# Transposes of 28 layer norm tiles: from TensorE to transposing transfers in SyncE's queue

## The chip, the cores and the metric

The kernel runs on the 8 cores of one Trainium2 chip. Each core computes one of the 8 batch items by itself; the cores exchange nothing. The metric is the device time of the slowest core in microseconds (us). The engines of a core are TensorE (PE; its weight loads are listed as PEld), VectorE (DVE), ScalarE (ACT), GpSimd (POOL) and SyncE (SP), which here only issues transfers (DMA).

## What is computed

For each batch item x of 2048 rows and 1024 columns: a gated feed-forward with half weight, an attention block with random features and its own MLP, and the same feed-forward again, each with a layer norm ahead of it.

```python
def _layernorm(x, axis=-1, eps=1e-5):
    m = jnp.mean(x, axis=axis, keepdims=True)
    v = jnp.var(x, axis=axis, keepdims=True)
    return (x - m) / jnp.sqrt(v + eps)
...
        gate = jnp.einsum('bsd,hd->bsh', x, wg)
        up = jnp.einsum('bsd,hd->bsh', x, wu)
        h = jax.nn.silu(gate) * up
        return jnp.einsum('bsh,dh->bsd', h, wd)

    x = x + 0.5 * _L0_ffn_ref(_layernorm(x, axis=-1), L0_ffn_w_gate, ...)
    x = x + _L0_attn_ref(_layernorm(x, axis=-1), ...)
    x = x + 0.5 * _L0_ffn_ref(_layernorm(x, axis=-1), L0_ffn_w_gate, ...)
    return x
```

Inside the attention block: q, k, v are x times Wq, Wk, Wv; q and k become exponential features of width 128 per head; a running state over the sequence gives the attention; then Wo, a residual, a second (inner) norm with gamma and beta, and relu(h W1 + b1) W2 + b2.

## The kernel before

**Tiling.** x stays in SBUF for the whole run as 16 tiles of 128 rows (x_tm). The 16 tiles are four blocks of 4 tiles (512 rows). Every matmul has a 512-wide right side, either 512 rows of activations with the features on the partitions (column groups: gate, up, q, k, w1) or 512 columns of weights (row groups: down, v, wo, w2).

**Norms.** Each block has three norms ahead of its three parts: LN1, LN2, LN3; besides, the inner norm of the attention block (called I). A tile of LN1, LN2 or LN3 passes through four steps. DVE takes statistics (L266 to L269, about 1.5 us) and POOL turns the variance into rstd. DVE writes the normalised tile in bf16 into one of the two halves of lntm (L297). PE transposes it in eight 128 x 128 pieces into one PSUM bank (L305). ACT copies the bank into its place in fmX, fmY or fmZ (L314), which is the activation operand of the next part. The tiles are numbered m = 0 to 47 in the order ln_order; a tile's half of lntm is m % 2, so normalisation m waits until tile m - 2 has been transposed (s_ltr). A part waits for the copies of its four tiles (s_lev).

**Weights.** All weights stream through a ring of 8 slots of 512 KB. SyncE issues the load of slot n when PE is done with slot n - 8 (sp_program, L699), one queue, in order. PE uses a slot for 16 matmuls, about 3.5 us, so a load is issued some 27 us ahead of its use. After three of the down parts SyncE also stores the four output tiles of a block.

**Order of the work.** Each engine has one hand-written program. A part of one block is the main stream on PE (gu, down, w1, w2, q, wo, k and v); side() is called after each group of matmuls and gives one tick to a side job: the attention steps of another block, norm tiles, or the inner norm. The same tick numbers are used on PE, DVE and ACT, with offsets, so that the engines meet. LN2 of blocks 1 to 3 is a side job inside the attention ticks (LN_STEP, one tile each at steps 29, 37, 45 and 53), where its transposes borrow the bank of the scores. LN3 of blocks 0 and 1 runs beside wo(1) and wo(2); LN3 of block 2 beside w1(3), of block 3 beside gu of block 2. After wo(b) comes kv_part(b + 1), beside which the inner norm I of block b is taken: dve_i_tick (statistics, then L355), pe_i_tick (transposes, L366, from the tick 5 of kv_part), act_i_tick (L375).

The evictions of wo(b) are on DVE (L1172, 8 per part, each 0.7 us); PE cannot start bank t of the next part before eviction t of the second half.

Of the kernel before, what the change touches and what calls it, by code (L numbers as in the profile page):

```python
# [40 lines left out]
def build():  # L41
# [29 lines left out]
    with es:  # L71
# [3 lines left out]
        def sem(name):  # L75
            return es.enter_context(nc.semaphore(name))
# [56 lines left out]
        s_lxf, s_ltr, s_lev = sem("s_lxf"), sem("s_ltr"), sem("s_lev")  # L133
        s_ixf, s_itr, s_iev = sem("s_ixf"), sem("s_itr"), sem("s_iev")
# [17 lines left out]
        def slot(n):  # L152
# [10 lines left out]
                    "I3", "32", "33"]  # L163

# [126 lines left out]
        def dve_ln_xform(e, which, b, j):  # L291
            n = st_no(which, b) + j
            m = ln_no(which, b) + j
            e.wait_ge(s_rstd, n + 1)
            if m >= 2:
                e.wait_ge(s_ltr, m - 1)
            e.tensor_scalar(lntm[:, (m % 2) * 1024:(m % 2 + 1) * 1024], xt(b * 4 + j),  # L297
                            mv[:, 2 * n:2 * n + 1], rstd[:, n:n + 1],
                            ALU.subtract, ALU.mult).then_inc(s_lxf, 1)

# [275 lines left out]
        def pe_attn(e, b, s):  # L576
            i, t0 = s // 2, 32 * b
            if s % 2 == 0:
                if i < 32:
                    pe_proj(e, t0 + i)  # L580
                if 0 <= i - 3 < 32:

                    if s - 1 in LN_STEP and b < 3:
                        e.wait_ge(s_lev, ln_no(LN2, b + 1) + LN_STEP.index(s - 1) + 1)
                    pe_scores(e, t0 + i - 3)
            else:
                if i >= 8 and i % 4 == 0:
# [12 lines left out]
                if s in LN_STEP and b < 3:  # L600
                    e.wait_ge(s_am, t0 + min(i - 2, 32))
                    pe_ln_transpose(e, LN2, b + 1, LN_STEP.index(s), 2)

        def act_attn(e, b, s):
            i, t0 = s // 2, 32 * b
            if s % 2:
                if i < 32:
                    act_exp(e, t0 + i)
            else:
                if 0 <= i - 2 < 32:  # L610
                    act_fme(e, t0 + i - 2)
                if i >= 9 and (i - 1) % 4 == 0:
                    act_oev(e, 8 * b + (i - 1) // 4 - 2)
                if s - 1 in LN_STEP and b < 3:
                    if s - 1 == LN_STEP[0]:
                        e.wait_ge(*((s_v, 16), (s_v, 32), (s_up, 120))[b])
                    act_ln_evict(e, LN2, b + 1, LN_STEP.index(s - 1), 2)
# [32 lines left out]
        def sp_program(e):  # L650
# [25 lines left out]
            store_at[first + 36 + 32 + 16 + 36 + 16 + 4 + 16 + 32 + 36 + 12] = 2  # L676
            for n in range(SL_GU2, len(slots)):
# [21 lines left out]
                e.dma_start(slot(n), src).then_inc(s_ld[n % RING], 16)  # L699
                if n in store_at:  # L700
# [86 lines left out]
        def pe_program(e):  # L787
# [73 lines left out]
            def gu(which, b, xT, side):  # L861
                e.wait_ge(s_lev, ln_no(which, b) + 4)
                for i in range(N_GU):
                    pair(next_slot(), xT, side)
# [4 lines left out]
            def q_part(b, xT, side):  # L869
                e.wait_ge(s_lev, ln_no(LN2, b) + 4)  # L870
# [82 lines left out]
            wo(1, Ticks(lambda k: pe_ln_tick(e, LN3, 0, k, 0, 1)))  # L953
# [9 lines left out]
            wo(2, Ticks(lambda k: pe_ln_tick(e, LN3, 1, k, 0, 1)))  # L963
# [17 lines left out]
        def act_program(e):  # L981
# [87 lines left out]

            def third(b, k):  # L1070
                if k == 0:
                    e.wait_ge(s_w1, 32 * (b + 1))
                act_ln_tick(e, LN3, b, k, 0, 1)
            idle(8, Ticks(lambda k: third(0, k)))
# [11 lines left out]
            idle(8, Ticks(lambda k: third(1, k)))  # L1086
# [11 lines left out]
            e.wait_ge(s_up, 144)  # L1098
            w1(3, Ticks(lambda k: act_ln_tick(e, LN3, 2, k, 0, 2)))
            e.wait_ge(s_w1, 96)  # L1100
            side = Ticks(lambda k: act_ln_tick(e, LN3, 3, k, 0, 4))
            gu(side)
            idle(24, side)
            gu(quiet)

        def dve_program(e):
# [123 lines left out]
            wo(1, Ticks(lambda k: dve_ln_tick(e, LN3, 0, k, 0, 1)))  # L1230
            side = Ticks(lambda k: dve_i_tick(e, 1, k))
# [10 lines left out]
            wo(2, Ticks(lambda k: dve_ln_tick(e, LN3, 1, k, 0, 1)))  # L1242
            side = Ticks(lambda k: dve_i_tick(e, 2, k))
# [122 lines left out]
```

## Time and profile before

| | us |
|---|---|
| median of 3 runs | 1841.48 |
| the runs | 1839.5, 1841.48, 1939.56 |
| the profiled execution, its own time | 1839.98 |
| its span on the slowest core (core 3) | 1838.3 |
| spans of the 8 cores | 1833.1 to 1838.3 |
| PE busy | 1798.1 (98%) |
| DVE busy | 777.5 (42%) |
| ACT busy | 533.1 (29%) |
| POOL busy | 186.3 (10%) |

How to read it: the span goes from the first to the last instruction of a core; the time around it (1.7 us here) belongs to the run and not to any instruction. PE's busy time is the union of its matmuls; their recorded durations overlap, so the cost of a few instructions is read from when the next one starts. A row of a timeline gives start, duration, engine, line, operation, tiles, form and count, and in brackets the idle time of the engine before it with what ended it. Times of a timeline count from the start of the span.

### The profile page before, as it was taken

How to read it: one execution, taken by the hardware profiler on the slowest of the kernel's cores; microseconds unless marked ns; L12 is line 12 of the kernel's file. 1: busy time of each engine (PE TensorE's matmuls, PEld its weight loads, DVE VectorE, ACT ScalarE, POOL GpSimd, SP SyncE). 2: the span in 40 equal slices, each digit the busy share in tenths (PEclk: the TensorE clock that was granted, in tenths of full speed). 3: DMA queues.
4: the chain of work that ended last, by engine and by line, in shares of the span. 5: the costliest groups of instructions: out<-in, count | busy, mean ns of one | idle time of the engine just before them, and what ended most of it. 6: DMA issues, size and time to landing. Idle time of an engine off the chain costs nothing.

```text
span 1838.3 us, 31579 instructions; the slowest of 8 cores (1833.1 to 1838.3 us)
## 1 busy us (share of the span) xinstructions
PE 1798.1 (98%) x10096; PEld 879.3 (48%) x10096; DVE 777.5 (42%) x1697; ACT 533.1 (29%) x1138; POOL 186.3 (10%) x354
## 2 busy tenths in 40 slices
PE   4999999999999999999999999999999999999999
PEld 2444444444445445554454454455554444444444
DVE  4443116511676345655554333566443120442331
ACT  2221002202454246543332541334352141120110
POOL 3111101100011131113000000300000200000000
PEclk9999999999999999999999999999999999999999
DMA  9999986999876843334444544443354444444643
GB/s 202 234 201 191 195 195 157 194 192 191 209 177 172 189 150 127 116 127 138 144 135 136 173 138 139 141 141 131 129 182 147 145 145 156 151 151 151 195 156 107
DMA packets 82235, 296.32 MB, mean 161 GB/s; under 512 B 9632, under 2 KB 9760, under 8 KB 82080
## 3 DMA queue, kind: packets, MB, share of 16 engines
q1 hardware_dynamic: 69552, 249.16, 41.3%
q0 software_dynamic: 12240, 44.11, 17.4%
q8 instruction: 90, 1.47, 0.3%
q10 hardware_dynamic: 288, 1.05, 0.2%
q14 instruction: 65, 0.53, 0.1%
HBM read 311.12 MB, written 52.43 MB: 198 GB/s over the span
## 4 chain that ended last, share of the span: by engine, by line
PE 94%; DMA 2%; DVE 1%; issue 1%; ACT 1%; POOL 0%; DVEq 0%; ACTq 0%; POOLq 0%; SPq 0%
PE d_ps L811 35%; PE d_ps L851 31%; PE d_ps L828 18%; PE a_ps L923 2%; PE d_ps L923 2%; DMA ring<-gu_b 2%; PE a_ps L451 1%; PE a_ps L305 1%; PE a_ps L498 1%; PE a_ps L412 1%; DMA x_tm<-xin 1%; PE a_ps L413 1%; PE a_ps L463 0%; PE a_ps L524 0%; ACT ftm L430 0%
## 5 line engine op out<-in xcount | busy, mean ns | idle before, releaser
L851 PE MATMUL d_ps<-ring,big 128*128 128x512 bf16 x2176 | 487.4, 379 | 0.8 <-DVE th_t L1116 0.7
L851 PEld LDWEIGHTS d_ps<-ring,big 128*128 128x128 bf16 x2176 | 207.1, 98 | 233.5 <-issue 2.3
L991 ACT ACTIVATE th_t<-d_ps 128x512 f32<-128x512 f32 x192 | 115.4, 601 | 590.6 <-PE d_ps L811 590.6
L811 PE MATMUL d_ps<-fmX,ring 128*128 128x512 bf16 x1152 | 266.4, 382 | 4.2 <-DMA ring<-gu_b 2.8
L811 PE MATMUL d_ps<-fmZ,ring 128*128 128x512 bf16 x1152 | 256.3, 379 | 0.0
L1116 DVE SCALAR_TENSOR_TENSOR th_t<-th_t,d_ps 128x512 f32<-128x512 f32 x192 | 131.8, 686 | 232.1 <-ACT th_t L991 232.0
L430 ACT ACTIVATE ftm<-a_ps,nmax 128x128 bf16<-128x128 f32 x512 | 146.9, 371 | 231.7 <-DVE nmax L420 231.7
L811 PEld LDWEIGHTS d_ps<-fmZ,ring 128*128 128x128 bf16 x1152 | 110.6, 98 | 125.6
L811 PE MATMUL d_ps<-fmY,ring 128*128 128x512 bf16 x768 | 169.2, 379 | 1.4 <-ACT fmY L314 1.4
L811 PEld LDWEIGHTS d_ps<-fmX,ring 128*128 128x128 bf16 x1152 | 109.6, 98 | 126.5 <-issue 8.6
L828 PE MATMUL d_ps<-fmX,ring 128*128 128x512 bf16 x640 | 144.9, 379 | 0.0
L828 PE MATMUL d_ps<-fmY,ring 128*128 128x512 bf16 x640 | 144.1, 379 | 0.0
L1121 DVE SCALAR_TENSOR_TENSOR big<-d_ps,th_t 128x512 bf16<-128x512 f32 x168 | 116.2, 692 | 49.4 <-PE d_ps L811 43.1
L1023 ACT ACTIVATE big<-d_ps,b1c_s 128x512 bf16<-128x512 f32 x128 | 88.8, 694 | 134.1 <-PE d_ps L828 133.7
L420 DVE TENSOR_REDUCE nmax<-a_ps 128x4 f32<-128x512 f32 x128 | 88.0, 687 | 87.6 <-PE a_ps L413 87.3
L811 PEld LDWEIGHTS d_ps<-fmY,ring 128*128 128x128 bf16 x768 | 75.0, 98 | 91.4 <-issue 1.5
L490 POOL CAST sb<-Sf 128x130 bf16<-128x130 f32 x120 | 38.9, 324 | 704.7 <-PE a_ps L529 635.0
L828 PEld LDWEIGHTS d_ps<-fmX,ring 128*128 128x128 bf16 x640 | 60.7, 98 | 67.0
L828 PEld LDWEIGHTS d_ps<-fmY,ring 128*128 128x128 bf16 x640 | 60.6, 98 | 66.8
L473 ACT COPY ffm<-a_ps 128x512 bf16<-128x512 bf16 x128 | 76.3, 596 | 38.5 <-PE a_ps L529 36.8
L1148 DVE SCALAR_TENSOR_TENSOR x_tm<-d_ps,x_tm 128x512 f32<-128x512 f32 x48 | 32.6, 689 | 118.7 <-PE d_ps L851 118.4
L1014 ACT ACTIVATE qkv<-d_ps 128x512 bf16<-128x512 f32 x64 | 38.3, 598 | 150.8 <-PE d_ps L828 150.8
(89 smaller groups left out, 1561.0 us busy)
## 6 DMA issues: line engine op xcount, KB each, us to landing
ring<-gu_b SPq DMA_DIRECT2D x144, 512.0 KB, 3.3
ring<-w_b SPq DMA_DIRECT2D x128, 512.0 KB, 3.2
ring<-d_b SPq DMA_DIRECT2D x72, 512.0 KB, 3.2
w_b<-w_f POOLq DMA_DIRECT2D x32, 512.0 KB, 9.3
ring<-gu_i POOLq DMA_DIRECT2D x24, 512.0 KB, 16.8
gu_b<-ring SPq DMA_DIRECT2D x24, 512.0 KB, 16.4
ring<-q_b SPq DMA_DIRECT2D x16, 512.0 KB, 4.1
ring<-k_b SPq DMA_DIRECT2D x16, 512.0 KB, 6.0
```

Source lines behind the costliest of these rows:

```text
L420: e.tensor_reduce(nmax[:, (t % 2) * 4:(t % 2) * 4 + 4], P_PS[:, :].rearrange("p (a b) -> p a b", a=4), axis=AX.X, op=ALU.max, negate=True) ...
L430: r = e.activation(ftm[:, o + j * 128:o + (j + 1) * 128], P_PS[:, j * 128:(j + 1) * 128], AF.Exp, bias=nmax[:, (t % 2) * 4 + j:(t % 2) * 4 ...
L473: e.copy(ffm[:, o:o + 512], T_BF[:, 0:512]).then_inc(s_fme, 1)
L490: e.tensor_copy(state_of(sb, t), state_of(Sf, t)).then_inc(s_sb, 1)
L811: r = e.matmul(d_ps[bank][:, :], ring[:, so + g * 1024 + k * 128:so + g * 1024 + (k + 1) * 128], xT[:, k * 512:(k + 1) * 512], start=(k == ...
L828: r = e.matmul(d_ps[bank][:, :], ring[:, so + j * 1024 + k * 128: so + j * 1024 + (k + 1) * 128], xT[:, k * 512:(k + 1) * 512], start=(k = ...
L851: r = e.matmul(d_ps[t][:, :], lhs[:, o:o + 128], ring[:, so + i * 512:so + (i + 1) * 512], start=(s == 0 and i == 0), stop=(s == n_slots - ...
L923: r = e.matmul(acc[:, :], (big, qkv)[t // 4][:, o:o + 128], ring[:, so + i * 512:so + (i + 1) * 512], start=(s == 0 and i == 0), stop=(s = ...
L991: e.activation(th_t[:, (n % 2) * 512:(n % 2 + 1) * 512], d_ps[2 * (n % 2)][:, :], AF.Tanh, scale=TANH_SC).then_inc(s_tanh, 1)
L1023: e.activation(big[:, f * 512:(f + 1) * 512], d_ps[f % 4][:, :], AF.Relu, bias=b1c[:, f:f + 1]).then_inc(s_relu, 1)
L1116: e.scalar_tensor_tensor(th_t[:, o:o + 512], th_t[:, o:o + 512], 1.0, d_ps[2 * (n % 2)][:, :], ALU.add, ALU.mult).then_inc(s_gm, 1)
L1121: e.scalar_tensor_tensor(dst, d_ps[2 * (n % 2) + 1][:, :], H_SC, th_t[:, o:o + 512], ALU.mult, ALU.mult).then_inc(s_h, 1)
```

## The change

From tile m = 20 on (XBAR0), that is for LN2 of blocks 1, 2 and 3 and for LN3 of all blocks, 28 tiles, the normalised tile is no longer transposed by PE and copied by ACT. SyncE issues one transfer from the half of lntm into the tile's place in fmX, fmY or fmZ, with transpose=True. These transfers stand in SyncE's queue of weight loads, each behind a load with a fixed number (turn_at). Ahead of each, SyncE waits until the tile is normalised (s_lxf), and for the first of a block also until the destination is free. Two new semaphores, one for each half of lntm (s_xb), count their landing; normalisation m waits on them instead of s_ltr, and the part that reads the tiles waits for both instead of s_lev. Tiles 0 to 19 stay as they were. In wo(1) and wo(2) DVE's ticks of the norm have stride 2 instead of 1, and reach into kv_part, where the ticks of the inner norm start in the same call.

```diff
+        XBAR0 = 20
...
             e.wait_ge(s_rstd, n + 1)
-            if m >= 2:
+            if m >= XBAR0 + 2:
+                e.wait_ge(s_xb[m % 2], 16 * ((m - XBAR0) // 2))
+            elif m >= 2:
                 e.wait_ge(s_ltr, m - 1)
...
+        def sp_ln_transpose(e, which, b, j):
+            m = ln_no(which, b) + j
+            dst = ln_order[m // 4][2]
+            e.wait_ge(s_lxf, m + 1)
+            if j == 0:
+
+                e.wait_ge(*((s_v, 16), (s_v, 32), (s_w1, 32), (s_up, 120), (s_w1, 64),
+                            (s_up, 144), (s_w1, 96))[m // 4 - XBAR0 // 4])
+            e.dma_start(dst[:, :].rearrange("p (k t) -> p k t", k=8)[:, :, j * 128:(j + 1) * 128],
+                        lntm[:, (m % 2) * 1024:(m % 2 + 1) * 1024],
+                        transpose=True).then_inc(s_xb[m % 2], 16)
+
+        def pe_ln_wait(e, which, b):
+            m = ln_no(which, b)
+            if m < XBAR0:
+                e.wait_ge(s_lev, m + 4)
+            else:
+                for j in range(2):
+                    e.wait_ge(s_xb[j], 32 * ((m - XBAR0) // 4 + 1))
...
-                    if s - 1 in LN_STEP and b < 3:
-                        e.wait_ge(s_lev, ln_no(LN2, b + 1) + LN_STEP.index(s - 1) + 1)
                     pe_scores(e, t0 + i - 3)
...
-                if s in LN_STEP and b < 3:
-                    e.wait_ge(s_am, t0 + min(i - 2, 32))
-                    pe_ln_transpose(e, LN2, b + 1, LN_STEP.index(s), 2)
...
-                if s - 1 in LN_STEP and b < 3:
-                    if s - 1 == LN_STEP[0]:
-                        e.wait_ge(*((s_v, 16), (s_v, 32), (s_up, 120))[b])
-                    act_ln_evict(e, LN2, b + 1, LN_STEP.index(s - 1), 2)
...
+            turn_at = {}
+            for which, b, at in ((LN2, 1, (105, 110, 114, 118)), (LN2, 2, (156, 160, 164, 168)),
+                                 (LN3, 0, (180, 181, 182, 183)), (LN2, 3, (217, 225, 232, 240)),
+                                 (LN3, 1, (264, 265, 266, 267)), (LN3, 2, (348, 349, 350, 351)),
+                                 (LN3, 3, (380, 382, 384, 386))):
+                for j in range(4):
+                    turn_at[at[j]] = (which, b, j)
...
                 e.dma_start(slot(n), src).then_inc(s_ld[n % RING], 16)
+                if n in turn_at:
+                    sp_ln_transpose(e, *turn_at[n])
...
             def gu(which, b, xT, side):
-                e.wait_ge(s_lev, ln_no(which, b) + 4)
+                pe_ln_wait(e, which, b)
...
-            wo(1, Ticks(lambda k: pe_ln_tick(e, LN3, 0, k, 0, 1)))
+            wo(1, quiet)
...
-            w1(3, Ticks(lambda k: pe_ln_tick(e, LN3, 2, k, 0, 2)))
+            w1(3, quiet)
...
-            wo(1, Ticks(lambda k: dve_ln_tick(e, LN3, 0, k, 0, 1)))
-            side = Ticks(lambda k: dve_i_tick(e, 1, k))
+            side = Ticks(lambda k: (dve_ln_tick(e, LN3, 0, k, 0, 2),
+                                    dve_i_tick(e, 1, k - 8)))
+            wo(1, side)
             idle(8, side)
             v_part(2, side)
```

ACT's ticks for these tiles (act_ln_tick, act_ln_evict) go in the same way, and wo(2) changes like wo(1).

PE's order in the second half of wo(1), first before and then with the change (the tile names are those of the code; L851 and L878 are the same matmul of row_groups):

```order
L851 MATMUL d_ps<-ring,fmZ 128x512 x15
L305 MATMUL a_ps<-ident,lntm 128x128 [waits s_lev,s_lxf]
L305 MATMUL a_ps<-ident,lntm 128x128 x7
L851 MATMUL d_ps<-ring,fmZ 128x512 [waits s_ld6,s_y]
L851 MATMUL d_ps<-ring,fmZ 128x512 x3
L851 MATMUL d_ps<-ring,fmZ 128x512 [waits s_y]
L851 MATMUL d_ps<-ring,fmZ 128x512 x3
L305 MATMUL a_ps<-ident,lntm 128x128 [waits s_lev,s_lxf]
```

```order
L878 MATMUL d_ps<-ring,fmZ 128x512 x15
L878 MATMUL d_ps<-ring,fmZ 128x512 [waits s_ld6,s_y]
L878 MATMUL d_ps<-ring,fmZ 128x512 x3
L878 MATMUL d_ps<-ring,fmZ 128x512 [waits s_y]
L878 MATMUL d_ps<-ring,fmZ 128x512 x3
```

The groups of eight transposes that stood between the matmuls are gone, with their waits for s_lxf and s_lev.

DVE's order in wo(1), from the first normalisation (L297, L303 after) of LN3 of block 0 to the first statistics of the inner norm; L1172 and L1187 are the evictions of wo. Before:

```order
L297 TENSOR_SCALAR lntm<-x_tm,mv,rstd 128x1024 [waits s_rstd,s_ltr]
L1172 SCALAR_TENSOR_TENSOR big<-x_tm,rstd,d_ps 128x512 [waits s_w2,s_rstd,s_wo]
L1172 SCALAR_TENSOR_TENSOR big<-x_tm,rstd,d_ps 128x512 [waits s_rstd,s_wo]
L266 BN_STATS bst<-x_tm 128x6 [waits s_w2x]
L267 BN_STATS bst<-x_tm 128x6
L269 BN_AGGR mv<-bst 128x2 [waits s_bst]
L297 TENSOR_SCALAR lntm<-x_tm,mv,rstd 128x1024 [waits s_rstd,s_ltr]
L1172 SCALAR_TENSOR_TENSOR big<-x_tm,rstd,d_ps 128x512 [waits s_rstd,s_wo] x2
L297 TENSOR_SCALAR lntm<-x_tm,mv,rstd 128x1024 [waits s_rstd,s_ltr] x2
L1172 SCALAR_TENSOR_TENSOR big<-x_tm,rstd,d_ps 128x512 [waits s_rstd,s_wo] x4
L266 BN_STATS bst<-big 128x6 [waits s_y]
```

And with the change, from the first evictions on:

```order
L1187 SCALAR_TENSOR_TENSOR big<-x_tm,rstd,d_ps 128x512 [waits s_rstd,s_wo] x3
L270 BN_STATS bst<-x_tm 128x6 [waits s_w2x]
L271 BN_STATS bst<-x_tm 128x6
L273 BN_AGGR mv<-bst 128x2 [waits s_bst]
L303 TENSOR_SCALAR lntm<-x_tm,mv,rstd 128x1024 [waits s_rstd,s_xb1]
L270 BN_STATS bst<-x_tm 128x6 [waits s_w2x]
L271 BN_STATS bst<-x_tm 128x6
L273 BN_AGGR mv<-bst 128x2 [waits s_bst]
L303 TENSOR_SCALAR lntm<-x_tm,mv,rstd 128x1024 [waits s_rstd,s_xb0]
L1187 SCALAR_TENSOR_TENSOR big<-x_tm,rstd,d_ps 128x512 [waits s_rstd,s_wo] x4
L303 TENSOR_SCALAR lntm<-x_tm,mv,rstd 128x1024 [waits s_rstd,s_xb1]
L270 BN_STATS bst<-big 128x6 [waits s_y]
```

Normalisations 1 and 2 move behind all four evictions of the first half, with a tile's statistics ahead of each, and normalisation 3 moves behind the last eviction, directly ahead of the inner norm's statistics.

SyncE's order with the change around LN3 of block 0 (L724 is the weight load that was L699; before, nothing stood between the loads):

```order
L724 DMA ring<-v_b 128x2048 [waits s_wo]
L316 DMA_TRANSPOSE fmX<-lntm 128x8x128 [waits s_lxf,s_w1]
L724 DMA ring<-v_b 128x2048 [waits s_wo]
L316 DMA_TRANSPOSE fmX<-lntm 128x8x128 [waits s_lxf]
L724 DMA ring<-v_b 128x2048 [waits s_wo]
L316 DMA_TRANSPOSE fmX<-lntm 128x8x128 [waits s_lxf]
L724 DMA ring<-v_b 128x2048 [waits s_wo]
L316 DMA_TRANSPOSE fmX<-lntm 128x8x128 [waits s_lxf]
L724 DMA ring<-gu_b 128x2048 [waits s_qk] x4
```

Each transposing transfer stands behind one v_b load and ahead of the next load, which goes out only after the transfer's own waits.

## Rows read from the trace of the kernel before

**Rows 1.** The page's first part: span, and busy time by engine.

```profile
span 1838.3 us, 31579 instructions; the slowest of 8 cores (1833.1 to 1838.3 us)
PE 1798.1 (98%) x10096; PEld 879.3 (48%) x10096; DVE 777.5 (42%) x1697; ACT 533.1 (29%) x1138; POOL 186.3 (10%) x354
```

**Rows 2.** Waits: engine, line, waited for: us in total, times, longest; last, a line's group.

```profile
PE a_ps L305 <- DVE lntm L297: 24.3, 4, 21.0
PE d_ps L811 <- DMA ring<-gu_b: 2.8, 2, 2.4
...
L498 PE MATMUL a_ps<-ffm 128*128 128x128 bf16 x256 | 35.1, 219 | 2.2 <-ACT fmX L314 1.2 <-ACT fmY L314 1.0
```

**Rows 3.** Busy time by engine, PE's clock, DMA share and GB/s, 515 to 1620 us.

```profile
515.00:1620.00 1105.00, 1097.75 (x6668) 553.84 (x6667) 509.75 (x1249) 408.21 (x916) 124.25 (x229) 1.00 0.46 146
```

**Rows 4.** The same stretch, with L305 alone (PE, PEld), then L314 alone (ACT).

```profile
515.00:1620.00 1105.00, 17.05 (x224) 14.07 (x224) 1.00 0.46 146
...
515.00:1620.00 1105.00, 28.53 (x28) 1.00 0.46 146
```

**Rows 5.** Timeline of PE in wo(1) and kv_part(2), start and us first.

```profile
834.61 0.61 PE L305 MATMUL a_ps<-ident,lntm 128*128 128x128 bf16 x8
835.06 1.89 PE L851 MATMUL d_ps<-ring,fmZ 128*128 128x512 bf16 x8
...
843.31 10.52 PE L828 MATMUL d_ps<-fmY,ring 128*128 128x512 bf16 x48
853.67 0.61 PE L366 MATMUL a_ps<-ident,big 128*128 128x128 bf16 x8
...
858.46 1.89 PE L851 MATMUL d_ps<-ring,fmY 128*128 128x512 bf16 x8
...
872.72 1.46 PE L811 MATMUL d_ps<-fmX,ring 128*128 128x512 bf16 x6
```

**Rows 6.** Timeline of PE at the last group of the stretch.

```profile
1613.49 0.61 PE L305 MATMUL a_ps<-ident,lntm 128*128 128x128 bf16 x8
1613.93 2.32 PE L811 MATMUL d_ps<-fmZ,ring 128*128 128x512 bf16 x10
```

**Rows 7.** Timeline of PE in the attention ticks of block 0.

```profile
543.25 0.27 PE L412 MATMUL a_ps<-omT,qkv 128*128 128x256 bf16 x1 [0.66 <-ACT ftm L430]
547.12 0.61 PE L305 MATMUL a_ps<-ident,lntm 128*128 128x128 bf16 x8 [1.11 <-DVE amT L508]
```

**Rows 8.** SyncE's loads in wo(1); transfers to landing there; 256 KB stores (median us last).

```profile
831.40 12.47 SPq L699 DMA_DIRECT2D ring<-v_b  x4
...
DMA to landing us min/median/max: 3.1/3.2/4.0
...
out<-x_tm SPq DMA_DIRECT2D x8, 256.0 KB, 2.1
```

**Rows 9.** DMA queue with the constants' small packets, 12.9 to 14.8 us: packets, MB, share.

```profile
q1 hardware_dynamic: 587, 0.10, 30.5%
```

**Rows 10.** L297 in 720 to 790 us: duration, first and last start.

```profile
L297 DVE TENSOR_SCALAR lntm<-x_tm,mv,rstd x4: 803/804/804, 729.8 to 781.5; 128x1024 bf16<-128x1024 f32 x4
```

**Rows 11.** Timeline of DVE in gu of block 2's third norm part.

```profile
1588.85 0.80 DVE L297 TENSOR_SCALAR lntm<-x_tm,mv,rstd 128x1024 bf16<-128x1024 f32 x1
...
1603.56 0.81 DVE L297 TENSOR_SCALAR lntm<-x_tm,mv,rstd 128x1024 bf16<-128x1024 f32 x1
```

**Rows 12.** Timeline of DVE in wo(1) and kv_part(2).

```profile
828.41 0.81 DVE L297 TENSOR_SCALAR lntm<-x_tm,mv,rstd 128x1024 bf16<-128x1024 f32 x1
832.30 1.61 DVE L1172 SCALAR_TENSOR_TENSOR big<-x_tm,rstd,d_ps 128x512 f32<-128x512 f32 x2 [3.08 <-PE d_ps L851]
833.83 0.69 DVE L266 BATCH_NORM_STATS2 bst<-x_tm 128x6 f32<-128x512 f32 x1
...
835.39 0.81 DVE L297 TENSOR_SCALAR lntm<-x_tm,mv,rstd 128x1024 bf16<-128x1024 f32 x1
...
844.43 0.69 DVE L266 BATCH_NORM_STATS2 bst<-big 128x6 f32<-128x512 f32 x1
...
850.41 5.00 DVE L355 TENSOR_SCALAR big<-big,mv,rstd 128x1024 bf16<-128x1024 f32 x4
```

More of the change, by code:

```diff
@@ L133, in build @@
         s_lxf, s_ltr, s_lev = sem("s_lxf"), sem("s_ltr"), sem("s_lev")
+        s_xb = (sem("s_xb0"), sem("s_xb1"))
         s_ixf, s_itr, s_iev = sem("s_ixf"), sem("s_itr"), sem("s_iev")
@@ L869, in q_part @@
             def q_part(b, xT, side):
-                e.wait_ge(s_lev, ln_no(LN2, b) + 4)
+                pe_ln_wait(e, LN2, b)
                 column_groups(xT, N_QK, s_qk, s_qke, 16 * b, side)
@@ L962, in pe_program @@
             q_part(3, fmX, side)
-            wo(2, Ticks(lambda k: pe_ln_tick(e, LN3, 1, k, 0, 1)))
+            wo(2, quiet)
             side = Ticks(lambda k: pe_i_tick(e, 2, k))
@@ L972, in pe_program @@
             w2(2, Ticks(lambda k: pe_i_tick(e, 3, k)))
-            w1(3, Ticks(lambda k: pe_ln_tick(e, LN3, 2, k, 0, 2)))
+            w1(3, quiet)
             w2(3, quiet)
-            side = Ticks(lambda k: pe_ln_tick(e, LN3, 3, k, 0, 4))
-            gu(LN3, 2, fmZ, side)
-            down(168, 48, side)
+            gu(LN3, 2, fmZ, quiet)
+            down(168, 48, quiet)
             gu(LN3, 3, fmY, quiet)
@@ L1068, in act_program @@
             qk(0, 2, side)
[L1070 to L1074, printed above, removed]
             side = Ticks(lambda k: act_i_tick(e, 1, k))
@@ L1085, in act_program @@
             qk(0, 3, side)
-            idle(8, Ticks(lambda k: third(1, k)))
             side = Ticks(lambda k: act_i_tick(e, 2, k))
@@ L1097, in act_program @@
             idle(32, Ticks(lambda k: act_i_tick(e, 3, k)))
[L1098 to L1103, printed above, removed]
+            w1(3, quiet)
+            gu(quiet)
             gu(quiet)
@@ L1241, in dve_program @@
             idle(8, side)
-            wo(2, Ticks(lambda k: dve_ln_tick(e, LN3, 1, k, 0, 1)))
-            side = Ticks(lambda k: dve_i_tick(e, 2, k))
+            side = Ticks(lambda k: (dve_ln_tick(e, LN3, 1, k, 0, 2),
+                                    dve_i_tick(e, 2, k - 8)))
+            wo(2, side)
             idle(8, side)
```

## The prediction

> **What bounds the kernel now.** I read the page's busy times first: PE is busy 1798.1 us of a span of 1838.3 [rows 1], so whatever leaves PE's stream shortens the run, as long as nothing new makes PE wait. The list of waits says how little PE waits: 24.3 us for the first four normalised tiles at the very start, and otherwise 2.8 us for weights and a few us for ACT and DVE [rows 2]. In the stretch from 515 to 1620 us, which holds everything that the change touches, PE is busy 1097.75 of 1105 us at a granted clock of 1.00 (full speed, 2.4 GHz), and the DMA engines are 0.46 busy [rows 3]. So in this stretch PE is the path, DMA has room, and a gain must be read from PE's own stream.
>
> **What is removed from PE.** The same window with only L305 in it counts 224 transposes, that is 28 groups of 8 [rows 4]. Its 17.05 us of busy time is not the price, since matmuls overlap; the price is how much later the next matmul starts. In wo(1) a group starts at 834.61 and the next matmul at 835.06, and the last group of the stretch is at 1613.49 with a matmul at 1613.93 [rows 5, 6]. That is 0.45 us each time, 28 x 0.45 = **12.6 us**. Two waits go with them. In the attention ticks the transposes use the bank of the scores, so PE waits for the mask first: 1.1 us in total, once [rows 7]. And the scores of the next tick wait for ACT's copy out of that bank: 1.2 us for fmX and 1.0 for fmY, **2.2 us** in four waits [rows 2]. ACT loses 28 copies of about 1.02 us [rows 4]; it waits for PE in this stretch, so they are worth nothing beyond the 2.2.
>
> Sum: 12.6 + 1.1 + 2.2 = 15.9 us, and 1840.0 (the profiled execution's own time, span 1838.3 plus 1.7 around it) - 15.9 = 1824.1. The median of the runs shown is 1.5 us above that execution, which makes 1825.6. I take **1825**.
>
> **What is added.** SyncE gets 28 transfers of 256 KB (128 x 1024 bf16). No row shows a transposing transfer, so its time T from issue to landing is bounded. Below: a 256 KB store lands in 2.1 us [rows 8]. A transfer in pieces of one destination row (128 values, 256 bytes) has 1024 pieces. Around 13 to 15 us the queue moves its small packets: 587 take 30.5% of 16 engines for 1.9 us, which is 0.305 x 1.9 x 16 / 587 = 15.8 ns each [rows 9]. So 1024 pieces need 1.0 us of all 16 engines, and T is about 3 us. Behind a weight load issued just ahead (3.2 us to landing in this stretch [rows 8]) it is 4 to 6 us. Above: if every 2-byte value were a piece, there would be 131,072 of them, 129 us of all engines. Between ends so far apart I take T = 3 to 6 us: the order lists one instruction of its own kind for a tile, its destination rows are contiguous, and so the row that it resembles is the small packets' row at 256 bytes.
>
> A rule of the Trainium skill bears on this (*DMA: Bandwidth & Descriptors*, Latency and other measured facts): a transposing transfer moves 261 GB/s where the middle dimension is not contiguous. By it the 256 KB take 1.0 us plus the landing time; the sum stays at 1825. No row here shows it.
>
> **What could wait for it.** Four parties, each with its slack.
> 1. *PE, for the transposed activations.* The last tile of each norm is issued at least seven slots ahead of its reader. In the third norm of block 0 it follows the last v_b load (about 843.5), and gu(LN3, 0) starts 29 us later, at 872.72 [rows 5]; free up to T = 25.
> 2. *The weight queue.* SyncE now stops for s_lxf. In wo(1) the loads go out at 831.4 and then about every 4 us [rows 8]; the first v_b slot is read at 858.46 [rows 5], 27 us after issue, against 3.2 to landing. What queues behind a waiting transpose are loads with over 20 us of cover, and one group of output stores (after slot 232), for which nobody waits.
> 3. *DVE, for lntm.* Its third write into the two halves waits for the first transfer. In the attention ticks of block 2, the closest ones, four tiles are spread from 729.8 to 781.5, 17 us apart [rows 10], so the third comes 34 us after the first: free up to about T = 30. In w1(3) DVE has nothing else to do. In gu(LN3, 2) the first normalisation starts at 1588.85 and the third at 1603.56 [rows 11]: free up to T = 13.8, counting from 1589.7, when the first ends.
> 4. *The tight place: wo(1), and wo(2) likewise.* I rebuild DVE's row order after the change with durations from [rows 12], in before's clock. Normalisation 0 ends at 829.2; transfer 0 is issued behind the load at 831.5. PE ends the first half at 834.6. DVE then evicts t3 (to 835.4), takes statistics 2 (1.5), normalisation 1 (0.8, to 837.7), statistics 3 (to 839.2), and wants normalisation 2, which needs transfer 0. The evictions of the second half follow; PE needs bank 0 at 841.5 (843.3 less the four groups' 1.8), so normalisation 2 must start by 840.0: T up to 8.5. Transfer 1 is issued at 837.8; DVE is ready for normalisation 3 after the last eviction, at 842.9: free up to T = 5.1. This one now stands ahead of the inner norm: 0.8 + four statistics 6.0 + first L355 1.25 end at 851.0. PE wants that tile at 853.67 - 1.8 = 851.9 (before, DVE had it at 851.7 for 853.67, 2 us early) [rows 5, 12]. So of 2 us of slack 0.9 are left, and PE waits once T passes about 6. Beyond it each of the two places costs T - 6.
>
> So the loss is 2(T - 6) for T over 6, plus 2(T - 13.8) over 13.8. At T = 3 to 6: 0. T = 10: 8. T = 14: 16, all of the gain. T = 23.4: 35 + 19 = 54, which is 2% above before.
>
> **Rivals.**
> *A. T is 6 to 14 us.* The tile is transposed block after block. For it: 128 x 1024 is eight square blocks, and nothing in the trace shows that the engines take them side by side. Against it: DMA engines are 0.46 busy, so there is room [rows 3]. Mechanism: DVE waits at normalisations 2 and 3 in wo(1) and wo(2), the inner norm is late, PE stops ahead of L366. At T = 10.5, 9 us come back: 1834. The Trainium skill has a figure on this side (*VectorE: DVE Perf Modes*, The three transpose paths): 1309 ns for a 128 x 128 bf16 transpose by DMA. Eight in series are 10.5 us and would give this 1834. No row shows which of the two rules holds for eight blocks in one instruction.
> *B. Slower.* T is over 14, because the transfer is cut finer than a destination row. It decides from T = 14 on, and at T = 30 it costs 48 + 32 = 80 us, less 15.9: 1906. At the 129 us of the upper bound the DMA engines alone would need 28 x 129 = 3.6 ms. For it: the source column of one destination row lies in 128 partitions, so every value comes from elsewhere. Against it: the instruction exists for the purpose.
> *C. The time freed in attention turns into waiting.* The twelve second-norm tiles sit between ticks whose features come from DVE and ACT; the short waits for ftm around 540 us show that this chain is near [rows 7]. If all twelve groups' 5.4 us and the 3.3 us of waits are swallowed, 7.2 remain: 1834. Against it: PE waits only 7.25 us in the whole stretch [rows 3].
> *D. More than 2% faster* would need 37 us. PE's whole idle time is 40.2, most of it in the first 50 us; there is nothing to get it from.
>
> **How the numbers follow.** Forecast (T up to 6, gain kept) 0.66, with its own range 1819 to 1829. A 0.15, C 0.04, giving 1829 to 1841. B 0.13: T of 14 to 23 (0.05) is up to 2% slower, above that (0.08) over 2% slower. D 0.02. What a measurement of this kernel can tell from no change is about 2%, 37 us. So faster 0.02, same 0.66 + 0.15 + 0.04 + 0.05 = 0.90, slower 0.08. The range leaves out T above 15 and D: 1819 to 1844, which holds about 0.85.
>
> **What the changed profile would show.** PE's instructions fall by 224, with no L305 row after 350 us, and ACT's copies L314 by 28. The new transfers' time to landing tells T: 3 to 6 us supports the sum, about 10 us rival A, over 14 rival B. In wo(1) and wo(2) PE should have no wait ahead of the inner norm's transposes, and none ahead of its first kv_part matmuls. PE should not wait for weights any longer than 2.8 us. In the attention ticks the waits for fmX and fmY are gone; if waits for ftm have grown by as much, it was C. DVE's waits at the normalisations should be near zero. Wrong would be a T over 6, a weight slot that lands late, or PE busy time that falls by much less than 12 us.

## The result: 15 us less, and the profile after

The changed kernel takes 1824.57 us (median; 1823.48 to 1826.84) beside 1839.74 before: ratio 0.9919, 95% interval 0.9909 to 0.9929, or 13.1 to 16.7 us. The prediction was 1825, in a range of 1819 to 1844. It counts as no change by the 2% bound, as forecast, and the interval lies clear of 1. One of the six executions of the kernel before (1939.56 us) was in a slower state that some executions of any kernel show, and every ratio here is taken without such executions.

The page of the changed kernel, its first part and its DMA packets (total; the queue that SyncE uses):

```profile
span 1822.3 us, 31070 instructions; the slowest of 8 cores (1818.0 to 1822.3 us)
PE 1783.2 (98%) x9872; PEld 866.1 (48%) x9872; DVE 776.2 (43%) x1697; ACT 504.7 (28%) x1110; POOL 187.1 (10%) x354
DMA packets 111802, 303.64 MB, mean 167 GB/s; under 512 B 39200, under 2 KB 39328, under 8 KB 111648
q1 hardware_dynamic: 99120, 256.50, 46.3%
```

Against [rows 1] the span is 16.0 us shorter; PE is busy 14.9 us less, with 224 matmuls fewer, and ACT 28.4 us less with 28 instructions fewer. SyncE's queue moves 99120 packets where it moved 69552; 29568 more are 28 times 1056, that is 1024 pieces for each tile (one for each destination row) and 32 other packets.

The waits of the changed kernel, in the columns of [rows 2]:

```profile
PE a_ps L332 <- DVE lntm L303: 24.3, 4, 21.0
PE a_ps L439 <- ACT ftm L457: 3.8, 8, 1.4
DVE lntm L303 <- DMA fmZ<-lntm: 3.6, 2, 3.3
PE d_ps L838 <- DMA ring<-gu_b: 2.9, 2, 1.7
```

What is missing matters most: no PE wait for the mask, none of the scores (L498 before) for ACT's copies, none for a transposing transfer, and the wait for weights is 2.9 us as it was 2.8. What is new on PE is small: the waits for ftm are 3.8 us in 8 places. Before, the same row (L412) was 1.5 us in 4.

The new transfers in the stretch of wo(1): SyncE's timeline first (start, us in the queue), then the time to landing of the four of wo(1), of the four in block 0's attention ticks (515 to 582 us), and of three that stand alone (720 to 770 us).

```profile
826.01 0.32 SPq L724 DMA_DIRECT2D ring<-v_b  x1
826.49 1.22 SPq L316 DMA_TRANSPOSE fmX<-lntm  x1
829.47 0.32 SPq L724 DMA_DIRECT2D ring<-v_b  x1
832.61 1.22 SPq L316 DMA_TRANSPOSE fmX<-lntm  x1
...
DMA to landing us min/median/max: 2.8/4.9/5.1
...
DMA to landing us min/median/max: 8.4/9.1/9.8
...
DMA to landing us min/median/max: 2.8/2.9/2.9
```

A transfer that stands alone lands in 2.8 us. Its 256 KB move in about 1.1 us of these: for the one issued at 727.26 us the traffic, in slices of 0.15 us, is 225 to 294 GB/s in six slices in a row, with 55 and 58 at their edges and nothing for a while on either side. In wo(1) the three that stand right behind a weight load landed in 4.8 to 5.1; the second, issued at 832.61, 3.1 us after the last load, landed in 2.8. Those of block 0's attention ticks, where POOL's casts run and the DMA engines are 0.94 busy, landed in 8.4 to 9.8 and held SyncE's queue for 1.3 to 2.7 us each. Over all 28 the median is 4.8 us.

DVE and PE at the tight place, wo(1) and the beginning of kv_part(2), in the changed kernel:

```profile
831.72 0.81 DVE L303 TENSOR_SCALAR lntm<-x_tm,mv,rstd 128x1024 bf16<-128x1024 f32 x1
834.73 2.72 DVE L1187 SCALAR_TENSOR_TENSOR big<-x_tm,rstd,d_ps 128x512 f32<-128x512 f32 x4
837.37 0.81 DVE L303 TENSOR_SCALAR lntm<-x_tm,mv,rstd 128x1024 bf16<-128x1024 f32 x1
844.07 5.00 DVE L382 TENSOR_SCALAR big<-big,mv,rstd 128x1024 bf16<-128x1024 f32 x4
822.33 13.97 PE L878 MATMUL d_ps<-ring,fmZ 128*128 128x512 bf16 x64 [1.03 <-ACT fmZ L596]
836.13 10.52 PE L855 MATMUL d_ps<-fmY,ring 128*128 128x512 bf16 x48
846.49 0.61 PE L393 MATMUL a_ps<-ident,big 128*128 128x128 bf16 x8
```

None of these rows of DVE has a wait in brackets. wo(1) is one unbroken run of 64 matmuls. The first tile of the inner norm is ready at 844.07 + 1.25 = 845.3 and PE takes it at 846.49, so 1.2 us of slack are left. Normalisation 3 (837.37) comes 4.8 us after the issue of transfer 1, which had landed 2 us earlier. So T could have grown to 4.8 before DVE waited, and to about 6.0 before PE did.

### The profile page after: what moved, and what is told of

The parts are those of the page before. It is cut to its first block, busy times and chain, and to the rows that moved or that the text cites. A ratio compares the mean times of both kernels' runs of the same rounds, so it can differ in the third digit from the quotient of the medians.

```text
span 1822.3 us, 31070 instructions; the slowest of 8 cores (1818.0 to 1822.3 us)
## 1 busy us (share of the span) xinstructions
PE 1783.2 (98%) x9872; PEld 866.1 (48%) x9872; DVE 776.2 (43%) x1697; ACT 504.7 (28%) x1110; POOL 187.1 (10%) x354
## 3 DMA queue, kind: packets, MB, share of 16 engines
q1 hardware_dynamic: 99120, 256.50, 46.3%
q0 software_dynamic: 12240, 44.11, 18.7%
## 4 chain that ended last, share of the span: by engine, by line
PE 94%; DMA 2%; DVE 1%; issue 1%; ACT 1%; POOL 0%; DVEq 0%; ACTq 0%; SPq 0%; POOLq 0%
PE d_ps L838 35%; PE d_ps L878 31%; PE d_ps L855 18%; PE a_ps L950 2%; PE d_ps L950 2%; DMA ring<-gu_b 2%; PE a_ps L478 1%; PE a_ps L439 1%; PE a_ps L525 1%; DMA x_tm<-xin 1%; PE a_ps L440 1%; ACT ftm L457 0%; PE a_ps L332 0%; PE a_ps L490 0%; PE a_ps L551 0%
## 5 line engine op out<-in xcount | busy, mean ns | idle before, releaser
L878 PE MATMUL d_ps<-ring,big 128*128 128x512 bf16 x2176 | 487.3, 379 | 0.8 <-DVE th_t L1131 0.7
L878 PEld LDWEIGHTS d_ps<-ring,big 128*128 128x128 bf16 x2176 | 206.9, 98 | 233.5 <-issue 2.3
## 6 DMA issues: line engine op xcount, KB each, us to landing
ring<-gu_i POOLq DMA_DIRECT2D x24, 512.0 KB, 16.3
```

Source lines behind the costliest of these rows:

```text
L878: r = e.matmul(d_ps[t][:, :], lhs[:, o:o + 128], ring[:, so + i * 512:so + (i + 1) * 512], start=(s == 0 and i == 0), stop=(s == n_slots - ...
```

## The experiments

A ratio is that of a kernel's runs to the runs of the kernel before on the same chip, with its 95% interval. Where a kernel is set against the changed one, 0.9919 is used if nothing else is said.

### Is the gain PE's instruction time?

One transpose in place of eight, in the kernel before. The copy keeps its size.

```diff
-            for k in range(8):
+            for k in range(8 if m < 20 else 1):
                 r = e.transpose(a_bf[bank][:, k * 128:(k + 1) * 128],
...
-                   a_bf[bank][:, :].rearrange("p (k t) -> p k t", k=8)).then_inc(s_lev, 1)
+                   a_bf[bank][:, :].rearrange("p (k t) -> p k t", k=8) if m < 20 else
+                   bass.AP(a_bf[bank], 0, [[1024, 128], [0, 8], [1, 128]])).then_inc(s_lev, 1)
```

> The kernel before, with one PE transpose in place of eight for each of the 28 tiles (the copy by ACT keeps its size and reads that one piece eight times; seven eighths of the transposed values are left out). Theory: the gain is PE's instruction time, 0.056 us each, so 28 x 7 x 0.056 = 11.0 us less than before (about 1829), with the waits for the mask and for ACT's copies still there (3 us). Rival C of the prediction (freed time in the attention ticks turns into waiting): 12 of the 28 groups bring nothing, so about 6 us less (1834), and the waits for ftm in the attention ticks grow by as much.

Measured: 0.9951 (0.9938 to 0.9965), which is 9.0 us less (6.4 to 11.4). The 11.0 of the theory lies inside; the 6 us of rival C lie just outside. The waits decide it, in the profile of this kernel:

```profile
PE a_ps L413 <- ACT ftm L431: 1.6, 4, 0.6
PE a_ps L499 <- ACT fmY L314: 1.3, 2, 0.8
PE a_ps L499 <- ACT fmX L314: 1.2, 2, 0.6
PE a_ps L305 <- DVE amT L509: 1.1, 1, 1.1
```

The waits for ftm have not grown (1.6 against 1.5), and the other three are there as in the kernel before. New in the changed stretch are 0.8 us in two places where PE waits for an eviction of wo; PE also waits longer for weights (5.4 us against 2.8), but before 500 us, where both kernels are the same. So all but 0.8 us of the freed instruction time stayed a gain.

The second kernel also copies only one eighth:

```diff
+            nk = 8 if m < 20 else 1
-            e.copy(dst[:, :].rearrange("p (k t) -> p k t", k=8)[:, :, j * 128:(j + 1) * 128],
-                   a_bf[bank][:, :].rearrange("p (k t) -> p k t", k=8)).then_inc(s_lev, 1)
+            e.copy(dst[:, :].rearrange("p (k t) -> p k t", k=8)[:, :nk, j * 128:(j + 1) * 128],
+                   a_bf[bank][:, :].rearrange("p (k t) -> p k t", k=8)[:, :nk, :]).then_inc(s_lev, 1)
```

> As the run with one transpose of eight, and ACT also copies only one eighth of the tile (seven eighths of the values are left out). Theory: the four waits of the scores for ACT's copy (2.2 us) go as well, so 13 us less than before in all, 2 us less than with one transpose alone. Rival: these waits are replaced by waits for ftm, which come from the same DVE and ACT chain; then it is equal to the other run within 1 us.

Measured: 0.9932 (0.9918 to 0.9945), 12.5 us less (10.1 to 15.1). The two intervals overlap, so the times don't separate the two kernels. The profile shows what happens to the waits:

```profile
PE a_ps L413 <- ACT ftm L431: 2.8, 6, 0.9
```

The 2.5 us for ACT's copies are gone, and the waits for ftm rise from 1.6 to 2.8. Both sides are half right: about half of what these waits gave back comes again one step later, from the chain of DVE and ACT that makes the features.

### What is a transposing transfer made of?

First the same transfer without transposing:

```diff
                         lntm[:, (m % 2) * 1024:(m % 2 + 1) * 1024]
-                        transpose=True).then_inc(s_xb[m % 2], 16)
+                        .rearrange("p (k t) -> p k t", k=8)).then_inc(s_xb[m % 2], 16)
```

> The changed kernel with plain transfers of the same size and the same 256-byte destination rows in place of the transposing ones (the transposition is left out, so the activations stay in row order). Theory: the transposing transfer's 4.8 us to landing are more than its 1024 pieces of 256 bytes need at 15.8 ns each (1.0 us of all engines); the plain one should land in 3 to 3.5 us and the queue should need about 0.3 us to issue it, against 1.22. Rival: the piece size alone sets it, then it also lands in 4.8 us. The time of the kernel is that of the changed kernel within 2 us in both cases, since PE waits for neither.

Measured: 0.9926 (0.9910 to 0.9941), the same as the changed kernel. The queue's row of eight plain transfers with the landing of all 28, then the landing of all 28 of the changed kernel (1.22 us of the queue, as above):

```profile
L316 SPq DMA_DIRECT2D fmX<-lntm x8: 605/606/606, 830.2 to 1060.3; - x8
DMA to landing us min/median/max: 2.7/4.3/9.1
```

```profile
DMA to landing us min/median/max: 2.7/4.8/9.8
```

The rival is nearly right: at the same piece size a plain transfer lands in 4.3 us against 4.8 (medians), and the quickest of both kinds in 2.7. Transposing costs 0.6 us more of the queue. The 0.5 us of landing is not clear of the differences between places: in wo(1) the plain ones have a median of 4.2 against 4.9, between 720 and 770 us 3.6 against 2.9. The theory's 3 to 3.5 us for the plain one left out the load ahead of it.

Then each tile as eight transfers:

```diff
-            e.dma_start(dst[:, :].rearrange("p (k t) -> p k t", k=8)[:, :, j * 128:(j + 1) * 128],
-                        lntm[:, (m % 2) * 1024:(m % 2 + 1) * 1024],
-                        transpose=True).then_inc(s_xb[m % 2], 16)
+            for k in range(8):
+                e.dma_start(dst[:, k * 512 + j * 128:k * 512 + (j + 1) * 128],
+                            lntm[:, (m % 2) * 1024 + k * 128:(m % 2) * 1024 + (k + 1) * 128],
+                            transpose=True).then_inc(s_xb[m % 2], 16)
```

The counts that DVE and PE wait for are eight times as large.

> The changed kernel with each tile's transfer cut into eight transposing transfers of 128 x 128. Rule of eight in series (Trainium skill, three transpose paths, 1309 ns each): the last lands 10.5 us after the first is issued, whatever the cut, and one of them alone needs 1.3 us; then 2 x (10.5 - 6) = 9 us slower than the changed kernel. Theory from the trace: the pieces are the same 1024, the eight differ by what the queue needs to issue them; at 0.4 us each (plain small transfers) the last lands after about 7 us, 2 us slower than the changed kernel; at 1.2 us each after 12 to 13 us, 13 us slower, all of it in wo(1) and wo(2).

Measured: 1.0158 (1.0140 to 1.0177), 44 us slower than the changed kernel, and more than any of the three numbers. SyncE's timeline in wo(1), DVE's normalisation 3 there, then three rows of the waits:

```profile
827.68 10.02 SPq L317 DMA_TRANSPOSE fmX<-lntm  x8
837.81 0.52 SPq L725 DMA_DIRECT2D ring<-v_b  x1
...
850.43 0.81 DVE L303 TENSOR_SCALAR lntm<-x_tm,mv,rstd 128x1024 bf16<-128x1024 f32 x1 [8.08 <-DMA fmX<-lntm]
...
PE a_ps L394 <- DVE big L383: 12.6, 2, 7.2
PE d_ps L856 <- DMA ring<-w_b: 11.7, 2, 7.6
PE d_ps L856 <- DVE big L1188: 6.1, 2, 3.0
```

A transfer of one block holds the queue for 1.25 us (10.02 / 8), and one of eight blocks for 1.22. So the queue's price is per instruction, not per block, and eight blocks in one instruction do not go one after the other at the price of one each. The cut takes 10 us of the queue for each tile. Normalisation 1 ended at 833.7, so T, from there to normalisation 3 at 850.4, was 16.7 us in wo(1) and 16.9 in wo(2), more than the 12 to 13 of the expectation. T - 6 is 21.6 us for both, and the transposes of the inner norm came 10.4 and 10.6 us later after the start of wo than in the changed kernel, 21.0; 18.7 us of it are the waits for the inner norm and for wo's evictions. Besides, PE waited 11.7 us for w1's weights (beside them the third norm of block 2 is taken), because the loads stood behind four tiles' transfers: the weight queue's cover of 27 us was used up by 40 us of queue time. For the weights of gu it waited 3.2 us more than in the changed kernel. The remaining 8 us fit the matmuls behind the long waits, which ran slower (this core's mean granted clock was 0.991); no run separates them.

### Is the slack count right?

More stores of 512 KB ahead of each of the eight transfers of wo(1) and wo(2), so that they land later (the scratch tensor padd and the semaphore s_pad are new, and SyncE waits for the stores only at its end):

```diff
+            if m in (28, 29, 30, 31, 36, 37, 38, 39):
+                for _ in range(3):
+                    e.dma_start(padd[n_pad[0]], b2r[:, :]).then_inc(s_pad, 16)
+                    n_pad[0] += 1
             e.dma_start(dst[:, :].rearrange("p (k t) -> p k t", k=8)[:, :, j * 128:(j + 1) * 128],
```

> The changed kernel with three more stores of 512 KB in the queue ahead of each of the eight transfers of wo(1) and wo(2) (third norm of blocks 0 and 1). Each store needs about 1.6 to 2 us of the DMA engines, so T goes from 4.9 to about 10 to 11 us. The prediction's slack count says 2 x (T - 6): 8 to 10 us slower than the changed kernel, with PE waiting ahead of the inner norm's transposes and for the evictions of wo. Rival (the slack count is wrong because DVE or the queue has cover that it overlooks): no more than 2 us slower.

Measured: 0.9998 (0.9985 to 1.0012), 14.5 us slower than the changed kernel: all of the gain. DVE and PE at wo(1):

```profile
830.19 0.81 DVE L306 TENSOR_SCALAR lntm<-x_tm,mv,rstd 128x1024 bf16<-128x1024 f32 x1
843.39 0.81 DVE L306 TENSOR_SCALAR lntm<-x_tm,mv,rstd 128x1024 bf16<-128x1024 f32 x1 [6.33 <-DMA fmX<-lntm]
820.80 13.97 PE L888 MATMUL d_ps<-ring,fmZ 128*128 128x512 bf16 x63 [1.03 <-ACT fmZ L605]
835.23 10.52 PE L865 MATMUL d_ps<-fmY,ring 128*128 128x512 bf16 x47 [0.46 <-DVE big L1197]
851.03 1.01 PE L402 MATMUL a_ps<-ident,big 128*128 128x128 bf16 x8 [5.28 <-DVE big L391]
852.27 3.08 PE L865 MATMUL d_ps<-fmY,ring 128*128 128x512 bf16 x7 [0.22 <-issue]
```

Transfer 1 was free to go at 831.0, when normalisation 1 ended, and let normalisation 3 start at 843.4: 12.4 us, stores included (10.4 from its own issue). T - 6 is 6.4, and the inner norm's transposes came 851.03 - 820.80 = 30.2 us after the start of wo(1), against 846.49 - 822.33 = 24.2 in the changed kernel: 6.1 later. PE waited 0.46 + 5.28 = 5.7 us here, and 12.6 in both places; in wo(2) T was 13.5 and the transposes came 7.1 later. That is the slack count to half a microsecond. What the expectation missed was the size of T and one more cost, the row behind the wait: seven matmuls in 3.08 us, where eight take 1.89. The granted clock there was 0.50, the lower of its two levels (1.2 GHz), and it cost about 2 us at each place. The sum, 13.2 + 4, is 17 us; the measured 14.5 has an uncertainty of about 3.

With six stores:

> As with three stores, with six: T about 15 to 17 us; by 2 x (T - 6) 18 to 22 us slower than the changed kernel, that is, no faster or a little slower than the kernel before. If the weight queue had less cover than counted (over 20 us), weights would come late too and it would be slower still, with PE waiting for ring slots in kv_part or gu.

Measured: 1.0092 (1.0076 to 1.0108), 32 us slower than the changed kernel. Normalisations 1 and 3 and PE at wo(1), then a table of stretches (the clock is the third number from the right), then the waits:

```profile
833.95 0.81 DVE L306 TENSOR_SCALAR lntm<-x_tm,mv,rstd 128x1024 bf16<-128x1024 f32 x1
854.76 0.81 DVE L306 TENSOR_SCALAR lntm<-x_tm,mv,rstd 128x1024 bf16<-128x1024 f32 x1 [9.11 <-DMA fmX<-lntm]
...
824.55 13.97 PE L888 MATMUL d_ps<-ring,fmZ 128*128 128x512 bf16 x63 [1.03 <-ACT fmZ L605]
843.82 1.01 PE L865 MATMUL d_ps<-fmY,ring 128*128 128x512 bf16 x2 [5.29 <-DVE big L1197]
845.05 11.95 PE L865 MATMUL d_ps<-fmY,ring 128*128 128x512 bf16 x45 [0.22 <-DVE big L1197]
862.40 1.01 PE L402 MATMUL a_ps<-ident,big 128*128 128x128 bf16 x8 [5.40 <-DVE big L391]
...
846.00:848.00 2.00, 2.00 (x6) 0.64 (x5) 0.00 (x0) 0.51 (x1) 0.00 (x0) 0.50 1.08 287
850.00:852.00 2.00, 2.00 (x11) 0.91 (x10) 0.00 (x0) 0.68 (x2) 0.00 (x0) 1.00 1.12 361
864.00:866.00 2.00, 2.00 (x6) 0.76 (x5) 2.00 (x1) 0.00 (x0) 2.00 (x2) 0.50 1.20 249
...
PE d_ps L865 <- DVE big L1197: 11.0, 3, 5.5
PE a_ps L402 <- DVE big L391: 10.4, 2, 5.4
```

PE waited 21.4 us, inside the 18 to 22 expected, and never for weights beyond the usual (3.3 us in all). But that it fell there is a coincidence, for T was not the 15 to 17 us that the range came from. Normalisation 1 ended at 834.8 and normalisation 3 started at 854.8: T was 20.0 us with the stores, and 20.1 in wo(2), so the slack count asks for 28 us in both places. And so late the inner norm's transposes came: 862.40 - 824.55 = 37.9 us after the start of wo(1) against 24.2, 13.7 later, and as much in wo(2).

PE's waits are 10.7 us of the 13.7. Most of the rest is slow matmuls between the two waits: the 48 matmuls ahead of the inner norm took 13.2 us (843.82 to 857.0), where they take 10.5. Behind each wait the granted clock was 0.50, and then 1.00 again. At a full clock PE would have waited so much longer at the inner norm, since DVE sets when that starts. Only the slow matmuls behind the second wait come on top, about 2 us at each place. The sum is 27.4 + 4 = 31 us, against 32 measured.

The control has the same six stores ahead of eight transfers in the attention ticks (tiles 24 to 27 and 32 to 35):

> Control: the same six stores ahead of eight transfers of the second norm of blocks 2 and 3, in the attention ticks. T is again about 15 to 17 us, but there the slack is 30 us: equal to the changed kernel within 2 us. If this is slower too, the stores cost by DMA traffic or queue time and not by the place.

There is no ratio for it; only its profiled execution can be set beside the others. It took 1823.97 us (the changed kernel 1824.57), and its spans were 1817.9 to 1822.4 us, those of the changed kernel 1818.0 to 1822.3. Its transfers of 720 to 800 us:

```profile
DMA to landing us min/median/max: 7.2/9.2/12.6
```

They landed in 7.2 to 12.6 us from their own issue. Counted as above, from the end of the normalisation and with the stores, T was 12.8 to 16.3 us, about what was expected, and no row of PE or DVE waits for them. The same stores cost 32 us in one place and nothing that this execution shows in the other.

### Was the new order of DVE's ticks needed?

```diff
-            side = Ticks(lambda k: (dve_ln_tick(e, LN3, 0, k, 0, 2),
-                                    dve_i_tick(e, 1, k - 8)))
-            wo(1, side)
+            wo(1, Ticks(lambda k: dve_ln_tick(e, LN3, 0, k, 0, 1)))
+            side = Ticks(lambda k: dve_i_tick(e, 1, k))
```

(and so in wo(2), in the changed kernel)

> The changed kernel with DVE's old order of the third norm's ticks in wo(1) and wo(2) (stride 1, nothing moved into kv_part). Theory from the measured landing of 4.9 us there: normalisation 3 waits for transfer 1, which can be issued about 835.5 on the clock of before and lands at 840.4, just before the evictions of the second half must start at 840.0 to 841; DVE waits 1 to 2 us there and PE at most 1 us at each place: equal to the changed kernel within 2 us. Rival: DVE's wait ahead of the evictions holds PE for the whole time to landing, 5 us at each place, 10 us slower than the changed kernel.

Measured: 0.9923 (0.9909 to 0.9936), equal to the changed kernel. DVE and PE in wo(1):

```profile
838.00 0.81 DVE L303 TENSOR_SCALAR lntm<-x_tm,mv,rstd 128x1024 bf16<-128x1024 f32 x1 [1.72 <-DMA fmX<-lntm]
835.04 5.34 PE L878 MATMUL d_ps<-ring,fmZ 128*128 128x512 bf16 x24 [0.50 <-DVE big L1187]
```

DVE waits 1.7 us for the transfer and PE 0.5 us for an eviction; wo(2) is alike, 1.0 us of PE's time in all. That is what the new order is worth in the trace, and the ratio is too coarse to show it.

### More tiles

Eight more tiles as transfers (second norm of block 0, first norm of block 3), PE's and ACT's ticks for them left out:

```diff
-        XBAR0 = 20
+        XBAR0 = 12
...
+            for which, b, at in ((LN2, 0, (44, 46, 48, 50)), (LN1, 3, (53, 55, 57, 59)),
+                                 (LN2, 1, (105, 110, 114, 118)), (LN2, 2, (156, 160, 164, 168)),
```

> The changed kernel with eight more tiles (second norm of block 0, first norm of block 3) as transposing transfers beside gu of block 2's first norm, behind slots 44 to 59. Theory: 8 x 0.45 = 3.6 us less than the changed kernel (about 1821 against 1824.6), if the transfers land within 14.7 us, the distance of the tiles m and m + 2. Rival: the DMA engines are 0.8 to 0.9 busy there with the casts of the weights, the transfers take over 15 us, DVE waits in the ticks of gu and PE behind it: no gain or a few us slower.

Measured: 0.9900 (0.9886 to 0.9913). The transfers beside the casts (285 to 350 us):

```profile
DMA to landing us min/median/max: 7.2/9.8/11.0
```

They landed in at most 11.0 us, under the 12.9 from the first one's issue (290.1) to the next but one normalisation (303.0), after which DVE would wait, and the spans are 1814.4 to 1820.9 against 1818.0 to 1822.3. The step of 0.0019 is the size of the 3.6 us, but its interval overlaps that of the changed kernel; this run alone doesn't show it.

The last three kernels ran together. The changed kernel once more:

> The changed kernel once more, beside the two below on the same chip: 0.992 of before again, 14 to 16 us less.

Measured: 0.9926 (0.9911 to 0.9941), 13.6 us less than the kernel before.

The inner norm's 16 tiles by transfers, with ACT scaling in place:

```diff
+        def sp_i_transpose(e, b, j):
+            e.wait_ge(s_ixf, 4 * b + j + 1)
+            if j == 0:
+                e.wait_ge(*((s_up, 96), (s_wo, 32), (s_wo, 48), (s_wo, 64))[b])
+            e.dma_start(c_buf[b][:, :].rearrange("p (k t) -> p k t", k=8)
+                        [:, :, j * 128:(j + 1) * 128],
+                        itm_of(b)[:, 8192 + j * 1024:8192 + (j + 1) * 1024],
+                        transpose=True).then_inc(s_ixb, 16)
...
-                e.wait_ge(s_itr, 4 * (b + 1))
+                e.wait_ge(s_ixb, 64 * (b + 1))
...
-                                 a_bf[f // 2][:, (f % 2) * 512:(f % 2 + 1) * 512], AF.Identity,
+                                 c_buf[b][:, f * 512:(f + 1) * 512], AF.Identity,
```

> The changed kernel with the inner norm's 16 tiles as transposing transfers too (behind the loads 10 and 11 slots after the start of the part beside them), ACT then scaling and shifting in place. Theory: 16 x 0.45 = 7.2 us less than the changed kernel, because a transfer that lands in 5 us behind DVE's last tile is followed by ACT's 5.5 us and still ends before w1 starts, and because PE no longer has to meet DVE there. Rival: in block 0, where w1 follows kv_part at once, the activations are late; w1 waits up to 5 us, which leaves a gain of 2 us; or the weight queue, stopped for DVE's tiles, lets a slot land late.

Measured: 0.9893 (0.9875 to 0.9911), 6.1 us less than the changed kernel beside it, for 7.2 expected; the intervals touch.

Both together:

> The same with the eight further tiles (second norm of block 0, first norm of block 3) as transfers: 7.2 + 3.6 = 10.8 us less than the changed kernel. Rival: the eight tiles bring less than 3.6, as the DMA engines are 0.8 to 0.9 busy there.

Measured: 0.9871 (0.9853 to 0.9889), against 0.9926 (0.9911 to 0.9941) for the changed kernel beside it: 10.1 us less, for 10.8 expected, with intervals apart, though this ratio and the one of the inner norm alone rest on two executions each. Against the kernel before it is 1.3%, 24 us. PE waits for the inner norm in block 0 only 0.3 us, not the 5 us of the rival:

```profile
669.79 1.89 PE L860 MATMUL d_ps<-fmX,ring 128*128 128x512 bf16 x8 [0.31 <-ACT fmX L400]
```

## Why the prediction was right, point by point

- **What bounds it.** PE in its own stream. One transpose of eight gave 9.0 us of the 11.0 expected (6.4 to 11.4), with 0.8 us of new waits in the changed stretch; more tiles brought about 0.45 us each (10.1 us for 24 tiles is 0.42).
- **The 12.6 us for 28 groups** held: PE has 224 instructions fewer, no wait but the one for ftm grew by more than 0.1 us, and the whole is 15.2 us by the medians. That the forecast of 1825 was met to 0.4 us is in part luck: the median of the kernel before was 1841.48 in the three runs that the sum started from and 1839.74 in six; from the first, the measured gain of 15.2 us would have led to 1826.3.
- **The 3.3 us of waits** was over-sized. The waits went, but those for ftm rose from 1.5 to 3.8, so that 1.0 remains. That is the small part of rival C that came true. The sum with it is 13.6; the medians give 15.2 and the interval 13.1 to 16.7, so the remaining difference can't be told from none.
- **T = 3 to 6 us** held for the places that matter (2.8 to 5.1 in wo(1)) and for the median, 4.8. The tight one, transfer 1 of wo(1), landed in 2.8, since it did not stand right behind a load. The bound from the small packets' row, 1.0 us a tile, is close to what came: the page counts 1024 pieces a tile, and a lone tile moved in about 1.1 us. Block 0's attention ticks had 8.4 to 9.8, and block 2's third norm up to 6.5. By the prediction's own sign ("wrong would be a T over 6") it was wrong there: it took the landing of a load in wo(1) for all places, and not the busier DMA engines of block 0's ticks. It cost nothing, because no reader waits for these tiles so soon.
- **The two readings of the Trainium skill.** Its *DMA: Bandwidth & Descriptors* (Latency and other measured facts) gives a transposing transfer 261 GB/s where the middle dimension is not contiguous. The trace agrees: 256 KB in about 1.1 us. Its *VectorE: DVE Perf Modes* (The three transpose paths) gives 1309 ns for a 128 x 128 transpose by DMA. The runs show that such figures do not add up over the blocks of one instruction: alone, a block costs 1.25 us of the queue and lands in 2.4 (median), and eight blocks in one instruction cost 1.22 and land in 2.8.
- **The four slacks.** PE waited for no transfer, the weight queue gave no late slot, DVE waited 3.6 us at two normalisations of block 2's third norm, where it has nothing else to do. The tight place had 1.2 us of slack left instead of 0.9. The loss beyond it, T - 6 for each place, was measured at 6.1 and 7.1 us for 6.4 and 7.5 with three stores, and at 13.7 for 14.0 with six.
- **The rival on the slower side** had its price a little too low. Its 2(T - 6) holds, but it left out the clock: PE waits of 5.0 us and more were each followed by matmuls at half rate, which adds about 2 us at each place. With T = 14 the gain was to be gone; with 12.4 and 13.5 it already was, within the 3 us that the measurement leaves open.

## What to carry to other kernels

If TensorE is busy 98% of the time, a transpose taken off it is worth the distance to the next matmul's start (0.45 us for eight), provided that someone with idle queue time can do it: here one transposing transfer of 128 x 1024 cost 1.22 us of SyncE's queue and 2.8 to 5 us to landing, and up to 2.7 and 9.8 us beside the casts. Put the whole tile into one instruction, and before placing it, rebuild the order on the engine that refills its source: the slack is there, and not at the reader of the result. Count for a new wait of some 5 us on TensorE about 2 us more than the wait itself.

## What was not expected of the hardware

- The queue's time for a transposing transfer is the same for one and for eight blocks of 128 x 128 (1.25 and 1.22 us, in wo(1)); a plain transfer with the same pieces takes 0.61, a weight load 0.32.
- After PE stood still for 5.0 us and more its granted clock was down: 0.50 in stretches of 2 us behind such waits, that is 1.2 instead of 2.4 GHz, and the matmuls right behind ran slower (seven in 3.08 us, against eight in 1.89). The Trainium skill says so too (*TensorE: Matmul & The Clock Gate*, Why this matters for your kernels: gaps between matmul bursts bring the lower clock back).
